# First attention step: another order of the splits on GpSimd and of the copied maxima on ScalarE

## What is computed

```python
qh = (q @ W_q).reshape(B, S, 16, 16)      # q = layernorm(x)
kh = (k @ W_k).reshape(B, S, 16, 16)      # k = v = ctx_1024
vh = (v @ W_v + b_v).reshape(B, S, 16, 16)
scores = jnp.einsum('bihd,bjhd->bhij', qh, kh) * scale
keep = (j < i) | (i == 0) & (j == 0)
probs = jax.nn.softmax(jnp.where(keep, scores, -jnp.inf), axis=-1)
attn = jnp.einsum('bhij,bjhd->bihd', probs, vh).reshape(B, S, HID)
x = x + attn @ W_o + b_o
```

## Time and profile before

| what | value |
|---|---|
| runs | 454.37 us median of 3 (450.68, 454.37, 456.5) |
| the profiled execution | 450.4 us, of which 448.3 us from the first to the last instruction (the span) |
| busy in the span | PE 83%, PEld 70%, DVE 65%, POOL 49%, ACT 42% |
| mean granted clock of TensorE | 0.933 of full speed |

### The profile page before, as it was taken

How to read it: one execution, slowest core, us unless ns; L and a number is a source line. 1 busy time by engine, 2 the same in 40 slices (tenths; PEclk the granted TensorE clock), 3 DMA queues, 4 the chain that set the end, 5 groups by cost and what they waited for, 6 DMA issues and landing times. The chain is left out here.

```text
span 448.3 us, 8117 instructions
## 1 busy us (share of the span) xinstructions
PE 372.3 (83%) x3026; PEld 315.8 (70%) x3026; DVE 293.1 (65%) x619; ACT 188.4 (42%) x255; POOL 220.0 (49%) x305
## 2 busy tenths in 40 slices
PE   3768699999999998766322799999999999999992
PEld 3736486767676766555211599999989898989891
DVE  5696376767676767523296666777776867777841
ACT  4424355555555553561140522526262626253310
POOL 7678557575757553250126810808171626350432
PEclk9999799999999999995555799999999999999997
DMA  6883716060606081323101611909181827330223
GB/s 212 229 235 74 195 28 186 28 188 27 188 4 188 3 245 53 110 82 107 47 1 59 236 35 11 263 24 263 30 251 39 232 62 215 81 48 10 25 35 34
DMA packets 36199, 49.10 MB, mean 110 GB/s; under 512 B 5022, under 2 KB 32064, under 8 KB 35136
## 3 DMA queue, kind: packets, MB, share of 16 engines
q1 hardware_dynamic: 27520, 34.91, 26.1%
q0 software_dynamic: 6144, 8.30, 9.9%
q10 hardware_dynamic: 2496, 5.38, 3.8%
HBM read 27.57 MB, written 8.39 MB: 80 GB/s over the span
## 5 line engine op out<-in xcount | busy, mean ns | idle before, releaser
L1256 POOL DMA_INDIRECT out_dram<-Y,scatter_idx x32 | 51.7, 1616 | 103.9 <-DVE Y L1414 88.1
L1298 ACT ACTIVATE hr<-ps,b_sb 128x512 f32<-128x512 f32 x64 | 43.3, 687 | 101.7 <-PE ps L1473 66.9
L635 DVE TENSOR_REDUCE nm<-ps 128x2 f32<-128x512 f32 (+1 forms) x96 | 61.5, 681 | 14.0 <-PE ps L822 13.9
L1483 PE MATMUL ps<-w_hi,h_hi 128*128 128x256 f32 x224 | 63.9, 285 | 1.9 <-DVE h_lo L1389 1.9
L1483 PE MATMUL ps<-w_lo,h_hi 128*128 128x256 f32 x224 | 63.4, 283 | 0.0
L1483 PE MATMUL ps<-w_hi,h_lo 128*128 128x256 f32 x224 | 63.4, 283 | 0.0
L453 ACT ACTIVATE PT<-ps 128x1536 f32<-128x1536 f32 x32 | 46.5, 1452 | 23.0 <-PE ps L838 22.0
L1387 DVE CAST h_hi<-hr 128x512 fp32r<-128x512 f32 x60 | 30.0, 499 | 38.7 <-ACT hr L1298 38.6
L1473 PE MATMUL ps<-XT_hi,w_hi 128*128 128x512 f32 x128 | 51.2, 400 | 1.5 <-DVE XT_lo L1376 1.5
L1473 PE MATMUL ps<-XT_hi,w_lo 128*128 128x512 f32 x128 | 50.9, 398 | 0.0
L1473 PE MATMUL ps<-XT_lo,w_hi 128*128 128x512 f32 x128 | 50.3, 393 | 0.0
(11 more groups left out here) (189 smaller groups left out, 865.2 us busy)
## 6 DMA issues: line engine op xcount, KB each, us to landing
raw<-in_L_ffn_w_dram SPq DMA_DIRECT2D x12, 1024.0 KB, 7.4
raw<-in_L_ffn_w_dram ACTq DMA_DIRECT2D x4, 1024.0 KB, 5.3
Ks<-k_h SPq DMA_DIRECT2D x24, 128.0 KB, 2.9
Qs<-q_h SPq DMA_DIRECT2D x24, 128.0 KB, 2.5
c_sb<-in_ctx_dram SPq DMA_DIRECT2D x8, 256.0 KB, 4.3
Ks<-k_m SPq DMA_DIRECT2D x16, 128.0 KB, 2.7
Qs<-q_m SPq DMA_DIRECT2D x16, 128.0 KB, 2.5
xn_rows<-x2n SPq DMA_DIRECT2D x8, 256.0 KB, 2.5
```

The source lines that it names most:

```text
L635: dve.tensor_reduce(nm[:, tile, h:h + count], max_bank[u % 2].rearrange("p (h j) -> p h j", h=count), AX_X, ALU.max, negate=True).then_inc ...
L1256: pool.indirect_dma_start(out_rows[:, :], bass.IndirectOffsetOnAxis(ap=scatter_idx[q][:, j:j + 1], axis=0), Y[q][:, j, :], None, bounds_ch ...
L1298: act.activation(hr[c % 2][:, :], h_bank[c % 4], ACT.Relu, bias=b1_sb[q][:, c:c + 1]).then_inc(hr_ready, 1)
L1483: last = pe.matmul(y_bank[j // 2][:, (j % 2) * D:(j % 2 + 1) * D], a[c % 4][:, j * P:(j + 1) * P], w[q][:, c, :], start=(c == 0 and n == 0 ...
```

## The change

Only step 0 differs, in two queues. On POOL the old order is `add_bias(2)`, `mask(0,0)`, `mask(0,1)`, `split_queries`, `split_keys`, `mask(0,2)`, `norm_powers(3)`, `mask(0,3)`. The new one puts the split of the queries ahead of `mask(0,1)`, keeps the split of the keys behind it, and puts `norm_powers(3)` last. On ACT the old order ends `exp(0,3)`, `norm_x(3)`, `values(0,1)`, `copy_maxima(0)`; the new one ends `exp(0,3)`, `copy_maxima(0)`, `values(0,1)`, `norm_x(3)`. `copy_maxima` carries one transfer, the 16 KB of L504. No instruction is added or removed, and no wait is changed. (The line `if s > 0` in front of `split_context` goes because step 0 now returns before it.)

```diff
             def step(s):
+                if s == 0:
+                    add_bias(2)
+                    mask(0, 0)
+                    split_queries(0)
+                    mask(0, 1)
+                    split_keys(0)
+                    mask(0, 2)
+                    mask(0, 3)
+                    norm_powers(3)
+                    return
                 if proj_part(s):
-                    if s > 0:
-                        split_context(s)
+                    split_context(s)
                     add_bias(s + 2)
                 if score_part(s):
                     mask(s, 0)
...
                     if score_part(s):
                         values(s, 0)
                         exp(s, 3)
-                    if s + 3 < B:
+                    if 0 < s and s + 3 < B:
                         norm_x(s + 3)
+                    if s == 0:
+                        copy_maxima(s)
                     if score_part(s):
                         values(s, 1)
-                    if max_part(s):
+                    if max_part(s) and s > 0:
                         copy_maxima(s)
+                    if s == 0:
+                        norm_x(3)
```

## The result

The changed kernel takes 449.68 us at the median of 20 runs, the kernel before 451.81 us at the median of 20. The ratio is 0.9927, with a 95% interval of 0.9905 to 0.9950: 3.3 us faster, between 2.3 and 4.3. (The ratio goes with the means of the runs, 452.74 and 449.58 us; the two medians lie only 2.1 us apart.) That is clear of the noise and well within 2%. The profiled execution took 450.07 us with a span of 447.9, only 0.4 us under the span of before. That is the puzzle of this case: as the next rows show, the step that was changed became 4.55 us shorter.

The account below looks back on a forecast made before the run. POOL's queue was taken to hold PE in step 0, with PE setting the pace afterwards. From 453.3 us, 4.3 us came off (2.4 order, 1.9 clock), forecast 449.0; range 445 to 454, the forecast's own 446 to 452.5.

Parts of the forecast that it names:

- What bounds step 0: Step 0: PE stalls 1.86 and 2.25 us, released by POOL's masks; it waits for POOL's queue, not for work.
- Part 1, the split: POOL, step 0: queries' split ahead of mask(0,1) takes 1.80 us (2.12 other end); mask(0,1) starts 0.35 us later, 42.3.
- Part 2: POOL, step 0: keys' split takes 1.80 us, mask(0,2) starts at 45.5; the 1.86 us stall ahead of values(0,2) goes.
- Part 3: POOL, step 0: mask(0,3) ahead of the powers starts at 47.81; values(0,3) follows at 49.29 instead of 51.92.
- What is late next: Step 0: both nm_s instructions on DVE finish only with the mask, 49.25; turn_maxima at 49.3, other end 48.4.
- From there to step 1: PE to step 1: full clock, turn_attention at 54.25, 4.3 us earlier; 2.4 us order, 1.9 us clock.
- a comparison of busy shares: PE's clock: held at 2.13 of 4 us busy (30 to 34 us), fell after 1.75 of 4 (46 to 50).
- ACT costed at nothing: ACT, steps 0 to 1: transfer lands at 53.2 to 53.8, hidden or 0.5 us late; xn has over 1 us cover.
- The step that failed: Middle of the attention: PE, busy 110.66 of 120 us, sets the pace, so gains ahead of it should be handed on.
- no gain arrives: Rival, chance 0.08: the stall only moves, or later steps wait for something that did not move; 453.3 us.
- slower: Rival, chance 0.05: clock falls in dense work of step 1 or later, up to 3.5 us each; two falls give 456.0.

Follow-up runs that it names:

- e2: ACT's new order alone, POOL keeping the old one, against the kernel before; ratio 0.9992.
- e5: The kernel before plus 16 extra matmuls that nobody reads in PE's two step 0 stalls; ratio 0.9996 to the kernel before.
- e1: POOL's new order alone, ACT keeping the old one, against the kernel before; ratio 0.9959.
- e6: The kernel before plus 54 extra matmuls that nobody reads in PE's idle times of steps 7 and 8; 448.18 us, ratio 0.9905.
- e7: The changed kernel plus the same extra matmuls in steps 7 and 8 as e6; 443.15 us, ratio 0.9800 to the kernel before.
- e8: e7 plus 58 more extra matmuls in the opening of the experts; 443.46 us, ratio 0.9808 to the kernel before.
- e4: The changed kernel with the powers left ahead of mask(0,3); ratio 0.9968 to the kernel before.

## Why the prediction was right, and where it was off

The time, 449.68 us, lies in the range, close to the 449.0 forecast. Two errors cancel in that: the forecast started from 453.3 us where 20 runs of the kernel before have a median of 451.81, and it took off 4.3 us where 3.3 were measured by the ratio and 2.1 by the medians. That the time came so close is luck. The profiled execution was forecast at 446.1 us and took 450.07: step 0 gave what was forecast, but it began 1.09 us later and the tail took 3.2 us back.

**What bounds step 0.** Right. POOL's queue held PE, and ACT's half alone (e2) is worth nothing.

**Part 1, the split.** Right. The queries' split took 1.81 us (41.56 to 43.37) against 1.80 forecast, and `mask(0,1)` started at 43.37 - 1.09 = 42.28 against 42.3.

**Part 2.** Right, with the longer split. The keys' split took 2.14 us (44.74 to 46.88), now the one beside DVE's `w_lo`; it stayed hidden, since `values(0,2)` waited for nothing.

**Part 3.** Right. `mask(0,3)` started at 48.88 - 1.09 = 47.79 against 47.81.

**What is late next.** The place was right and its price went. DVE's two small instructions:

```profile
49.04 0.18 DVE L699 CAST nm_s<-nm 128x32 bf16<-128x32 f32 x1
49.25 0.53 DVE L701 TENSOR_TENSOR nm_s<-nm,nm_s 128x32 bf16<-128x32 f32 x1
```

The first ran free and only the second was held up, so `turn_maxima` came before the end of the mask and `values(0,3)` waited for the mask: 50.40 - 1.09 = 49.31, the 49.29 of part 3 rather than 49.5. The Trainium skill, SBUF — State Buffer, section "Who interferes with whom", says that the order of issue decides who is blocked. The rows agree with it: 0.18 us for the instruction that began at 49.04, where POOL passed from one select of the mask to the next, and 0.53, against a median of 0.193, for the one that came behind the start of that select.

**From there to step 1.** The sum was right, 4.55 us against 4.3, with the clock at 1.00 as forecast. The split between order and clock, which the prediction drew at the start of `values(0,3)`, came out near the 2.4 and 1.9 forecast: 51.92 - 49.31 = 2.61 us ahead of it, and 6.65 - (55.11 - 50.40) = 1.94 behind. On the old order the clock alone is worth less, 1.5 us (e5), since the transfer then holds PE. The reason given for the clock, a comparison of busy shares, does not carry (e1).

**ACT costed at nothing.** Right: `b_scores(1,0)` started at 54.14 without a wait. ACT's timeline:

```profile
50.62 0.63 ACTq L513 DMA_DIRECT2D Qs<-nmT  x1
...
52.25 1.09 ACT L446 ACTIVATE xn<-x_all,rs 128x256 f32<-128x256 f32 x2 [0.28 <-POOL rs L330]
```

`xn` was done at 53.34, more than 2 us ahead of its use. e1 shows what that part of the change keeps away, 2.1 us.

**The step that failed** is in the first paragraph of the prediction: that what PE gains ahead of the dense stretch should be handed on. It was, through 170 us. Behind that the profile of before showed a tail in which PE idles often, and the prediction's sum has no term for it. In the two profiles of the changed kernel T to R was 3.2 and 1.3 us longer than before. The rival "no gain arrives" had the right outline, a loss behind step 0, but named other causes. The rival "slower" named the cause, a later fall of the clock, and placed it in dense work; its one fall, which leaves 4.3 - 3.5 = 0.8 us, comes nearest to the first profile, in which 1.4 us were left. It had 0.05. e6 and e7 show the cause: with the clock held in the tail, nearly the whole gain of step 0 arrives at the experts. Why the clock falls earlier in some executions than in others is left open; no run here settles it.

## What to carry to other kernels

An engine that is 49% busy can hold the one that matters for a few microseconds by the order of its queue alone; look at what stands ahead of each instruction that the bounding engine waits for, and at what the moved work then makes late on the next engine. A gain made early must be followed to the end of the trace, landmark by landmark: a thin stretch behind it, in which PE idles often, can give it back through the clock, as steps 7 and 8 did here. Where two kernels differ by less than such a stretch costs, compare the way between two landmarks and not the spans, and try PE-filling matmuls in the thin stretch: here they were worth 1% by themselves, and with them the change was worth 4.8 us by the ratios instead of 3.3 (3.6 between landmarks instead of 1.4 and 3.2). The best kernels of this case are e7, at 443.15 us, and e8, at 443.46, which the runs do not tell apart.

## What the runs showed of the hardware that was not expected

- The tail's clock falls at different places in executions of the same kernel: T to R was 167.73 and 165.87 us in two profiles of the changed kernel, where M to T differed by 0.01 us.
- It fell with short idle times: in step 0 of e4 it fell at 50.5 us, inside an idle time of PE of 1.79 us, and from 43 us on none before it was longer than 0.42 us.
- 54 extra matmuls that nobody reads, placed in idle times, made the kernel before 3.8 us faster at the median (448.18 against 451.99 of the kernel before beside it), by the ratio 4.3 us.
- A DVE cast of 128x4 elements lasted 6.30 us beside POOL's 5.63 us of bfloat16 products (e8); over the six times that this line ran there its median is 0.16 us.
